# One core, a selective scan on VectorE: the product B x of the next step is issued ahead of the scan of this step

## Chip, cores and metric

The kernel runs on one core of one Trainium2 chip. The time is device time in microseconds (us) from launch to the last result, the median of several runs. Beside the times there is one profiled execution; its trace gives every instruction's start and duration on TensorE (PE), VectorE (DVE), ScalarE (ACT), GpSimd (POOL) and the DMA queues, counted from the start of the span.

## What is computed

Eight sequences of 512 tokens with 256 channels go through a state-space layer and then a layer of eight experts, all in float32. The part that matters is the scan of the first layer, for 512 inner channels and 16 state indices:

```python
dt = softplus(dt_in @ dt_proj_w.T + dt_proj_b)
A = -exp(A_log)
def step(state, inp):
    dt_t, B_t, C_t, x_t = inp
    state = exp(A[None] * dt_t[:, :, None]) * state + B_t[:, None, :] * x_t[:, :, None]
    y = einsum('bnd,bd->bn', state, C_t) + D * x_t
    return (state, y)
# x_t = silu(conv(layernorm(x) @ in_proj_w.T)); B, C, dt_in are projections of it
out = silu(y) @ out_proj_w.T + shortcut
# then: x1 = x + layernorm(out); x1 + layernorm(shared expert + chosen expert of layernorm(x1))
```

## The kernel before, in words

The 512 inner channels lie on 128 partitions in 4 chunks; time is the free dimension. The recurrence is independent for each channel and state index, so it is one scan instruction over time per (half of the channels, state index). I call one sequence a **pass**: 8 passes of Q = 32 **steps**, step q = (half q // 16, state index q % 16), each on tiles of 128 x 1024. Passes 0, 1, 6 and 7 are written out; passes 2 to 5 are two rounds of a dynamic loop with two passes each. For a step q:

- *decay q* (ACT, line 763, two instructions): exp(A dt) into PSUM, two buffers. It waits until scan q-2 is done.
- *product q* (B times x): 15 of 32 on POOL (line 500, the even q but 22), 17 on DVE (line 1078, the odd q and 22), into four buffers. DVE's product reads B from PSUM, where TensorE's *spread q* has put it over all partitions (line 1486, one buffer: spread q waits for the DVE product before it). POOL's product reads B from a tile loaded by DMA.
- *scan q* (DVE, line 1090): waits for product q, decay q, and for the state buffer of eight steps ago.
- *weighing q* (POOL, line 511): state times C, waits for scan q.
- *sum q* (TensorE, line 1529): adds weighed states in PSUM, waits for weighing q.

The order on each engine is written out by hand, per step q. On POOL: product q+4 if it is POOL's (it waits for scan q, because of the four buffers), then weighing q; at q = 20 also `loss` (line 516), a part of the softplus for the next pass. On ACT: decay q+2, then what the step has of other work. On TensorE: spread q+2, sum q-3, then other work.

The other work belongs to the next pass (`front`) and to the pass before (`back`). Of `front`: at q = 2, 4, 6, 8 ACT starts one convolution chunk (line 654), and at q = 3, 5, 7, 9 DVE adds its three taps (line 1025); at q = 10 ACT makes the SiLU behind decay 12; projections on TensorE at q = 11 and 14 (lines 1413, 1419); softplus on ACT at q = 12 to 22; at q = 23 and 24 DVE takes a minimum (line 1039) after ACT's square (line 688), which waits for `loss`; at q = 25 to 28 TensorE sums dt and ACT copies it (line 694). Of `back`: at q = 2 ACT copies y (line 753); at q = 15 and 17 TensorE does the output projection (line 1451), which waits for `front`'s projection to leave the bank; at q = 16 and 18 DVE adds it to the residual (line 1048) and takes statistics (line 1006). In pass 7 the shared expert of sequence 0 (`early`, lines 1507, 739, 1068) takes the place of `front`: its gate copies on ACT stand at q = 1 to 4, behind decay q+2. After pass 7 come the experts, which use none of this.

Of the kernel before, what the change touches and what calls it, by code (L numbers as in the profile page):

```python
# [19 lines left out]
def build(nc, x, winT, conv_w, xprojT, dt_w, dt_b, A_log, D, woutT, norm_w, norm_b,  # L20
# [47 lines left out]
    with ctx:  # L68
# [914 lines left out]
        def _(dve):  # L983
# [29 lines left out]
            def lead(f, par, q):  # L1013
                if q == 10:
                    dve.wait_ge(x_loaded, 16 * (f + 1))
                    if not (isinstance(f, int) and f < 2):
                        dve.wait_ge(mv_ready[0], f - 1)
                    stats(0, cl, f, xin, mv0[par], mv0_ready)

            def front(f, par, q):  # L1020
                if q in (3, 5, 7, 9):
                    c = q // 2 - 1
                    dve.wait_ge(tap_done, C * f + c + 1)
                    for m in range(1, TAPS):
                        last = nc.vector.scalar_tensor_tensor(  # L1025
                            out=acc[:, c, m:L], in0=psF[:, 0:L - m],
                            scalar=cw[:, c, TAPS - 1 - m:TAPS - m], in1=acc[:, c, m:L],
                            op0=ALU.mult, op1=ALU.add)
                        if m == TAPS - 1:
                            last.then_inc(conv_done, 1)  # L1030
                        else:
                            cf.link(f, last)
                if q in (23, 24):


                    h = slice(0, 2) if q == 23 else slice(2, 4)
                    dve.wait_ge(loss_ready, f + 1)
                    dve.wait_ge(sq_ready, f + 1)
                    nc.vector.scalar_tensor_tensor(out=lt[:, h], in0=lt[:, h], scalar=LN_MARGIN, in1=dt[par][:, h],
                                                   op0=ALU.add, op1=ALU.min).then_inc(min_done, 1)  # L1040

            def back(b, q):
                if q in (16, 18):
                    h = q // 2 - 8
                    dve.wait_ge(h0_ready, b + 1)
                    dve.wait_ge(oproj_ready, 2 * b + h + 1)
                    half = ao[:, 2 * h:2 * h + 2].rearrange("p a c -> p (a c)")
                    nc.vector.tensor_tensor(half, psF[:], half, ALU.add).then_inc(ao_done, 1)
                if q == 18:
                    dve.wait_ge(ao_done, 2 * b + 2)  # L1050
                    stats(1, cb, b, ao, mv[1], mv_ready[1])
                if q in (22, 24):
                    h = q // 2 - 11
                    if h == 0:
                        dve.wait_ge(xres_loaded, 16 * (b + 1))
                    dve.wait_ge(x1_normed, 2 * b + h + 1)
                    rows = slice(2 * h, 2 * h + 2)
                    nc.vector.tensor_tensor(ao[:, rows].rearrange("p a c -> p (a c)"), psF[:],
                                            xr[:, rows].rearrange("p a c -> p (a c)"),
                                            ALU.add).then_inc(x1_half, 1)  # L1060
                if q == 25:
                    dve.wait_ge(x1_half, 2 * (b + 1))
                    stats(2, cb, b, ao, mv[2], mv_ready[2])

            def early_act(c):
                dve.wait_ge(e_silu, 1)
                dve.wait_ge(e_up, c + 1)
                nc.vector.tensor_tensor(acc[:, c], psF[:], acc[:, c], ALU.mult).then_inc(e_act, 1)

            def choose(b):  # L1070
                dve.wait_ge(logit_ready, b + 1)
                nc.vector.tensor_copy(logits[:, bass.ds(b * J, J), :].rearrange("p j e -> p (j e)"),
                                      psF[:, 0:J * E]).then_inc(logit_kept, 1)

            def inject(i, par, q):
                h, n = divmod(q, N)
                dve.wait_ge(b_bcast, i * DQ + NTH_D[q] + 1)
                nc.vector.tensor_tensor(bx[q % RB][:], xh[par][:, h * CH:(h + 1) * CH],  # L1078
                                        psB[:].unsqueeze(1).broadcast_to([P, CH, L]), ALU.mult).then_inc(dve_bx, 1)

            def scan(i, q):
                k = i * Q + q
                if BY_POOL[q]:
                    dve.wait_ge(pool_bx, i * PQ + NTH_P[q] + 1)
                else:
                    dve.wait_ge(dve_bx, i * DQ + NTH_D[q] + 1)
                dve.wait_ge(decay_ready, k + 1)
                if not (isinstance(k, int) and k < RS):
                    dve.wait_ge(summed, k - RS + 1)
                nc.vector.tensor_tensor_scan(st[q % RS][:].rearrange("p c t -> p (c t)"),  # L1090
                                             decay[q % RD].rearrange("p c t -> p (c t)"),
                                             bx[q % RB][:].rearrange("p c t -> p (c t)"),
                                             0.0, ALU.mult, ALU.add).then_inc(scanned, 1)

            def iteration(i, par, do_lead, do_front, do_scan, do_back, do_choose=True):
                for q in range(Q):
                    if do_scan:
                        scan(i, q)
                        if q + 1 < Q and not BY_POOL[q + 1]:
                            inject(i, par, q + 1)  # L1100
                    if do_scan and not do_front and q in (12, 13, 14, 15):
                        early_act(q - 12)
                    if do_back:
                        back(i - 1, q)
                    if do_choose and q == 20:
                        choose(i - 2)
                    if do_front:
                        front(i + 1, 1 - par, q)
                    if do_lead:
                        lead(i + 2, par, q)  # L1110
# [42 lines left out]

            first_front()
            iteration(0, 0, True, True, True, False, False)
            iteration(1, 1, True, True, True, True, False)
            with dve.Fori(2, NB - 3, 2) as i:
                iteration(i, 0, True, True, True, True)
                iteration(i + 1, 1, True, True, True, True)
# [37 lines left out]
            oh, cnt, incl, q = rt["oh"], rt["cnt"], rt["incl"], rt["q"]  # L1197
# [543 lines left out]
```

## Time and profile before

| | us |
|---|---|
| median of 3 runs (1410.88 to 1412.58) | 1411.01 |
| the profiled execution, its time | 1411.09 |
| its span, first to last instruction | 1409.3 |
| busy PE / DVE / ACT / POOL | 1175.4 / 1089.8 / 770.9 / 1088.4 |
| DVE: 256 scans, 2279 ns each | 578.5 |
| DVE: 136 products, 1196 ns each | 162.7 |
| POOL: 256 weighings, 2398 ns each | 606.6 |
| POOL: 120 products, 2426 ns each | 291.1 |

DVE and POOL are busy in over nine tenths of nearly every slice from 45 to 992 us, the eight passes, and TensorE afterwards. A row of a timeline gives the start in us, the time to the end of the group in us, engine, line, operation, tile written and tiles read, and how many instructions are merged; in brackets, where the engine sat idle before it, how long and what ended that. Instructions of one engine overlap slightly: two scans in a row start 2.20 us apart.

### The profile page before, as it was taken

The page shows a single profiled execution, that of the slowest core. Times are in us where ns is not written, and L with a number is a line of the kernel's source. Part 1 is how long each engine was busy: PE and PEld are TensorE (multiplying, and loading weights), DVE is VectorE, ACT ScalarE, POOL GpSimd, SP SyncE. Part 2 cuts the span into 40 slices and gives each one's busy share as a digit, 9 for nine tenths or more (in the row PEclk, how much of TensorE's full clock was granted, in tenths as well). Part 3 has the DMA queues.
Part 4 walks back from the last instruction along what each step waited for, and adds up shares of the span by engine and source line. Part 5 has one row for each costly group of instructions (what it writes and reads, how often), then busy time and mean ns, then how long its engine had stood idle before and what let it go on. Part 6 is the DMA issues. An engine that isn't in the chain of part 4 may idle for free.

```text
span 1409.3 us, 15754 instructions
## 1 busy us (share of the span) xinstructions
PE 1175.4 (83%) x4782; PEld 518.5 (37%) x4783; DVE 1089.8 (77%) x1449; ACT 770.9 (55%) x1275; POOL 1088.4 (77%) x565
## 2 busy tenths in 40 slices
PE   5667678787886987888789688788999999999996
PEld 2222223222321422322233142233556655566653
DVE  3599999999999999999999989799241115776675
ACT  5757468676876866867686686556431111111111
POOL 0489999999999999999999999999122814444553
PEclk9898899999899999989998999999999999999998
DMA  3921211240150122014015012300269522222220
GB/s 108 274 68 62 90 60 32 75 150 0 65 192 1 62 91 106 32 75 149 1 66 175 1 62 90 134 0 31 90 238 324 162 71 82 81 81 79 83 67 15
DMA packets 72075, 127.71 MB, mean 91 GB/s; under 512 B 8759, under 2 KB 48448, under 8 KB 67904
## 3 DMA queue, kind: packets, MB, share of 16 engines
q1 hardware_dynamic: 60432, 103.72, 22.2%
q0 software_dynamic: 7152, 16.81, 3.7%
q10 hardware_dynamic: 4416, 6.29, 1.3%
q8 instruction: 33, 0.54, 0.2%
q14 instruction: 42, 0.34, 0.1%
HBM read 97.79 MB, written 31.76 MB: 92 GB/s over the span
## 4 chain that ended last, share of the span: by engine, by line
PE 36%; POOL 29%; issue 15%; DVE 12%; ACT 8%; DMA 0%; POOLq 0%; ACTq 0%; SPq 0%; DVEq 0%
POOL state L511 18%; PE psX L1647 10%; POOL bx L500 9%; DVE state L1090 6%; PE psX L1582 5%; PE psY L1595 3%; PE psY L1664 2%; PE bank L1664 2%; PE psY L1529 2%; PE bank L1451 2%; POOL lt L516 2%; ACT psX L763 2%; PE bank L1486 1%; DVE bx L1078 1%; DVE acc L1025 1%
## 5 line engine op out<-in xcount | busy, mean ns | idle before, releaser
L511 POOL TENSOR_TENSOR state<-state,cbc 128x1024 f32<-128x1024 f32 x256 | 606.6, 2398 | 14.9 <-DVE state L1090 14.8
L1090 DVE TENSOR_TENSOR_SCAN state<-psX,bx 128x1024 f32<-128x1024 f32 x256 | 578.5, 2279 | 38.5 <-ACT psX L763 23.1
L763 ACT ACTIVATE psX<-dt,aneg 128x511 f32<-128x511 f32 x512 | 330.7, 679 | 199.0 <-DVE state L1090 197.6
L500 POOL TENSOR_TENSOR bx<-xh,bbc 128x1024 f32<-128x1024 f32 x120 | 291.1, 2426 | 59.5 <-DMA bbc<-bc_rows 43.1
L1529 PE MATMUL psY<-state,ident 64*64 64x512 f32 x2048 | 287.5, 654 | 20.3 <-POOL state L511 20.0
L1486 PE MATMUL bank<-prow,ident 128*128 128x512 f32 x272 | 169.9, 710 | 113.3 <-DVE bx L1078 113.3
L1078 DVE TENSOR_TENSOR bx<-xh,bank 128x1024 f32<-128x1024 f32 x136 | 162.7, 1196 | 7.7 <-PE bank L1486 7.6
L1529 PEld LDWEIGHTS psY<-state,ident 64*64 64x64 f32 x2048 | 63.9, 140 | 206.8 <-issue 126.2
L961 ACT ACTIVATE sg<-psX 128x512 f32<-128x512 f32 x39 | 23.3, 597 | 196.5 <-PE psX L1647 196.5
L1486 PEld LDWEIGHTS bank<-prow,ident 128*128 128x128 f32 x272 | 48.0, 209 | 206.9 <-DVE bx L1078 166.9
L581 POOL DMA_INDIRECT ysl<-shared_rows,idx x39 | 40.3, 1033 | 80.6 <-DVE idx L1258 75.9
L1167 DVE TENSOR_TENSOR actS<-sg,psX 128x512 f32<-128x512 f32 x28 | 19.0, 686 | 103.6 <-ACT sg L911 103.6
L1647 PE MATMUL psX<-wg,xsT 128*128 x156 | 77.2, 617 | 1.3 <-DVE xsT L1243 0.6
L1647 PE MATMUL psX<-wu,xsT 128*128 x156 | 73.3, 592 | 0.0
L1406 PE MATMUL bank<-lt,win 128*128 128x512 f32 x112 | 55.5, 618 | 15.7 <-DVE acc L1025 14.4
L590 POOL DMA_INDIRECT result<-yo,idx x39 | 40.1, 1029 | 36.8 <-DVE yo L1306 29.3
L1025 DVE SCALAR_TENSOR_TENSOR acc<-bank,cw,acc 128x511 f32<-128x511 f32 (+2 forms) x84 | 62.3, 742 | 3.3 <-ACT acc L654 1.2
L561 POOL COPY xrow<-ids 128x4 f32<-128x4 f32 x8 | 1.6, 203 | 77.6 <-issue 55.1
L1249 DVE TENSOR_TENSOR actN<-sg,psX 128x512 f32<-128x512 f32 x39 | 26.8, 688 | 44.1 <-ACT sg L961 41.6
L1451 PE MATMUL bank<-wout,yv 128*128 128x256 f32 x256 | 58.5, 381 | 2.0 <-ACT yv L709 1.9
L911 ACT ACTIVATE sg<-psX 128x512 f32<-128x512 f32 x28 | 16.5, 596 | 76.8 <-PE psX L1582 76.8
L1582 PE MATMUL psX<-xg,shg 128*128 128x512 f32 x112 | 53.1, 596 | 1.8 <-DVE actS L1167 1.8
(200 smaller groups left out, 1718.8 us busy)
## 6 DMA issues: line engine op xcount, KB each, us to landing
cbc<-bc_rows SPq DMA_DIRECT2D x32, 1024.0 KB, 5.0
bbc<-bc_rows SPq DMA_DIRECT2D x16, 1024.0 KB, 6.2
slot_in<-ao SPq DMA_DIRECT2D x1, 5011.5 KB, 35.1
xsl<-slot_in SPq DMA_DIRECT2D x39, 128.5 KB, 2.0
xin<-in_x SPq DMA_DIRECT2D x8, 512.0 KB, 4.5
xr<-in_x SPq DMA_DIRECT2D x8, 512.0 KB, 5.5
x_rows<-ao SPq DMA_DIRECT2D x8, 512.0 KB, 2.9
xn_rows<-xr SPq DMA_DIRECT2D x8, 512.0 KB, 3.2
```

The costliest lines, as they stand in the source:

```text
L500: nc.gpsimd.tensor_tensor(bx[q % RB][:], xh[par][:, h * CH:(h + 1) * CH], bbc[:, n // 2].unsqueeze(1).broadcast_to([P, CH, L]), ALU.mult). ...
L511: nc.gpsimd.tensor_tensor(w[:], w[:], cbc[:, n].unsqueeze(1).broadcast_to([P, CH, L]), ALU.mult).then_inc(weighted, 1)
L763: e = nc.scalar.activation(decay[q % RD][:, c, 1:L], dt[par][:, h * CH + c, 1:L], ACT.Exp, scale=aneg[:, h * CH + c, n:n + 1])
L1025: last = nc.vector.scalar_tensor_tensor(out=acc[:, c, m:L], in0=psF[:, 0:L - m], scalar=cw[:, c, TAPS - 1 - m:TAPS - m], in1=acc[:, c, m:L ...
L1078: nc.vector.tensor_tensor(bx[q % RB][:], xh[par][:, h * CH:(h + 1) * CH], psB[:].unsqueeze(1).broadcast_to([P, CH, L]), ALU.mult).then_inc ...
L1090: nc.vector.tensor_tensor_scan(st[q % RS][:].rearrange("p c t -> p (c t)"), decay[q % RD].rearrange("p c t -> p (c t)"), bx[q % RB][:].rea ...
L1451: last = nc.tensor.matmul(psF[:, (j % 2) * DIM:(j % 2 + 1) * DIM], yv[:, c, j * P:(j + 1) * P], wout[:, c], start=(c == 0), stop=(c == C - 1))
L1486: nc.tensor.matmul(psB[:], ident[:, n:n + 1].broadcast_to([P, P]), prow[par][:], start=True, stop=True).then_inc(b_bcast, 1)
L1529: done = nc.tensor.matmul(psY[o * HP:(o + 1) * HP, r], weights(half, c), src[half, c], start=first, stop=last_)
L1582: last = nc.tensor.matmul(bank, w[:, k, c * P:(c + 1) * P], xg[g % 2][:, k], start=(k == 0), stop=(k == KC - 1))
L1647: last = nc.tensor.matmul(bank, xsT[i][:, k], w[:, bass.ds(ereg[i], 1), k].rearrange("p a n -> p (a n)"), start=(k == 0), stop=(k == KC - 1))
L1664: last = nc.tensor.matmul((psF, psG)[i][:, 0:DIM], actT[i][:, c], wd[:, bass.ds(ereg[i], 1), c].rearrange("p a n -> p (a n)"), start=(c == ...
```

## The change

For each step q that has a DVE product behind it, the product for step q+1 is put ahead of scan q instead of behind it. What follows scan and product in the step (`back`, `front`) stays behind both. The order was scan 0, product 1, scan 1, scan 2, product 3, scan 3; it becomes product 1, scan 0, scan 1, product 3, scan 2, scan 3. At q = 21 and 22 it becomes product 22, scan 21, product 23, scan 22.

```diff
             def iteration(i, par, do_lead, do_front, do_scan, do_back, do_choose=True):
                 for q in range(Q):
                     if do_scan:
-                        scan(i, q)
                         if q + 1 < Q and not BY_POOL[q + 1]:
                             inject(i, par, q + 1)
+                        scan(i, q)
                     if do_scan and not do_front and q in (12, 13, 14, 15):
                         early_act(q - 12)
                     if do_back:
```

## Rows read from the trace of the kernel before

**Rows 1.** Chain that ended last, shares of the span by engine.
```profile
PE 36%; POOL 29%; issue 15%; DVE 12%; ACT 8%; DMA 0%; POOLq 0%; ACTq 0%; SPq 0%; DVEq 0%
```
**Rows 2.** Who waited for whom, POOL for DVE: us in total, times, longest.
```profile
POOL bx L500 <- DVE state L1090: 16.4, 8, 5.6
POOL state L511 <- DVE state L1090: 14.8, 9, 3.0
```
**Rows 3.** Timeline of POOL, pass 3: weighing 19, product 24, `loss`.
```profile
484.32 2.35 POOL L511 TENSOR_TENSOR state<-state,cbc 128x1024 f32<-128x1024 f32 x1 [1.44 <-DVE state L1090]
486.64 2.35 POOL L500 TENSOR_TENSOR bx<-xh,bbc 128x1024 f32<-128x1024 f32 x1
...
491.26 4.54 POOL L516 TENSOR_TENSOR lt<-lt,dt 128x2048 f32<-128x2048 f32 x1
```
**Rows 4.** Chain that ended last, pass 5 to 6: start us, us, what.
```profile
726.65 4.56 POOL lt L516
...
804.92 0.67 ACT psX L763
...
837.89 2.36 POOL state L511
```
**Rows 5.** Timeline of DVE: product 11 and statistics; product and its scan, pass 6.
```profile
450.68 1.20 DVE L1078 TENSOR_TENSOR bx<-xh,bank 128x1024 f32<-128x1024 f32 x1
451.79 1.40 DVE L1006 BATCH_NORM_STATS2 bst<-xin 128x6 f32<-128x256 f32 x4
...
788.49 1.20 DVE L1078 TENSOR_TENSOR bx<-xh,bank 128x1024 f32<-128x1024 f32 x1
789.72 2.29 DVE L1090 TENSOR_TENSOR_SCAN state<-psX,bx 128x1024 f32<-128x1024 f32 x1
```
**Rows 6.** Timeline of DVE, pass 3: scans 0 to 3, product 3, first taps.
```profile
410.65 2.29 DVE L1090 TENSOR_TENSOR_SCAN state<-psX,bx 128x1024 f32<-128x1024 f32 x1 [1.25 <-ACT psX L763]
...
414.26 4.47 DVE L1090 TENSOR_TENSOR_SCAN state<-psX,bx 128x1024 f32<-128x1024 f32 x2 [0.21 <-DVE bx L1078]
418.65 1.20 DVE L1078 TENSOR_TENSOR bx<-xh,bank 128x1024 f32<-128x1024 f32 x1
420.05 2.29 DVE L1090 TENSOR_TENSOR_SCAN state<-psX,bx 128x1024 f32<-128x1024 f32 x1 [0.21 <-DVE bx L1078]
422.26 2.29 DVE L1025 SCALAR_TENSOR_TENSOR acc<-bank,cw,acc 128x511 f32<-128x511 f32 x3
```
**Rows 7.** Timeline of ACT, pass 3: decay 4, first tap's activation, decay 12.
```profile
418.76 1.30 ACT L763 ACTIVATE psX<-dt,aneg 128x511 f32<-128x511 f32 x2 [0.18 <-DVE state L1090]
...
421.16 0.69 ACT L654 ACTIVATE acc<-bank,cw 128x512 f32<-128x512 f32 x1
...
450.79 1.30 ACT L763 ACTIVATE psX<-dt,aneg 128x511 f32<-128x511 f32 x2 [3.10 <-DVE state L1090]
```
**Rows 8.** Timeline of PE: spread 31 of pass 2, spread 3 of pass 3.
```profile
404.32 1.02 PE L1486 MATMUL bank<-prow,ident 128*128 128x512 f32 x2
...
414.78 1.02 PE L1486 MATMUL bank<-prow,ident 128*128 128x512 f32 x2
```
**Rows 9.** Timeline of DVE, pass 3: scans 19 and 20.
```profile
481.99 4.43 DVE L1090 TENSOR_TENSOR_SCAN state<-psX,bx 128x1024 f32<-128x1024 f32 x2
```
**Rows 10.** Timeline of DVE, line 1039: the minimum in pass 0 and pass 3.
```profile
142.04 8.26 DVE L1039 SCALAR_TENSOR_TENSOR lt<-lt,dt 128x1024 f32<-128x1024 f32 x1 [1.13 <-ACT dt L688]
...
497.85 1.35 DVE L1039 SCALAR_TENSOR_TENSOR lt<-lt,dt 128x1024 f32<-128x1024 f32 x1 [0.34 <-ACT dt L688]
```
**Rows 11.** Timeline of DVE, pass 7: products 3 and 7.
```profile
891.81 1.22 DVE L1078 TENSOR_TENSOR bx<-xh,bank 128x1024 f32<-128x1024 f32 x1 [4.06 <-PE bank L1486]
...
906.17 1.22 DVE L1078 TENSOR_TENSOR bx<-xh,bank 128x1024 f32<-128x1024 f32 x1
```
**Rows 12.** Timeline of ACT, pass 7: decays 12 and 28.
```profile
917.55 1.30 ACT L763 ACTIVATE psX<-dt,aneg 128x511 f32<-128x511 f32 x2 [0.88 <-DVE state L1090]
...
974.22 1.30 ACT L763 ACTIVATE psX<-dt,aneg 128x511 f32<-128x511 f32 x2 [2.59 <-DVE state L1090]
```

## The prediction

> **What bounds the kernel now.** I read the chain that ended last first: its largest single engines are TensorE, then GpSimd [rows 1]. TensorE's share is mostly the expert part after 995 us, which the change does not touch, so only the eight passes of the scan (about 45 to 992 us) count. There the list of who waited for whom shows that GpSimd waits for VectorE for only 31 us in all [rows 2]: GpSimd's own work (weighings, its products, one `loss`) fills nearly the whole stretch, and a faster VectorE alone can win back no more than those 31 us.
>
> The question is what ends GpSimd's waits. In each of passes 1 to 6 there is one of 1.4 to 3.0 us in front of weighing 19; the shortest is shown [rows 3]. Weighing 19 waits for scan 19, product 24 behind it for scan 20, then comes weighing 20 and then `loss`. The chain shows, from pass 5 to pass 6, how this closes into a ring [rows 4]: from `loss` at 726.65 it leaves GpSimd, runs through ScalarE, TensorE and VectorE (softplus, dt, start of the pass, convolution taps, SiLU at 804.92, projections, statistics) and is back at weighing 19 at 837.89. So a pass lasts as long as this ring from `loss` to `loss`, and GpSimd's own work in it is 1.4 to 3.0 us shorter. Whatever moves a station of the ring moves the end, six times over.
>
> **The change.** It removes and adds no instruction: 136 products, 17 a pass, are issued one scan earlier. The scan that used to run ahead of such a product (the even ones, mostly) now runs behind it. No DMA moves, and no queue of SP or GpSimd changes. The product's own wait (for TensorE's spread of B) now stands ahead of the even scan, and behind that scan queue ScalarE's next decay, GpSimd's product q+4 and weighing q.
>
> (a) *What is saved.* Where the odd scan directly follows its own product, it starts 1.40 us after the product's start in the dynamic loop [rows 6] and 1.23 us in the passes written out [rows 5]. An instruction that doesn't need the product starts 1.11 us after it [rows 5]. In the new order the even scan follows and doesn't need it, so I take 1.40-1.11 = about 0.28 us saved per product in passes 2 to 5 and 0.12 in the others. The end on the other side is no saving at all: nothing in the trace shows a scan behind a product of another step. I take the saving because statistics behind a product, of which there is a row, stand nearest.
>
> The Trainium skill ("VectorE: DVE Perf Modes", section "The DRAIN you can't avoid") says that a semaphore after each VectorE instruction costs nothing extra, which would make (a) nil. The rows show 0.12 and 0.28 us, so I follow the rows; its case is a rival below.
>
> (b) *Scans 0 to 3 and the first tap, worked on pass 3.* At the end of pass 2, product 31 can start when its spread is there, 404.32+1.02 = 405.3 [rows 8]. Scan 30, which was done by then, must now follow: 405.4+1.1+2.2 = 408.7, scan 31 to 410.9, product 1 to 412.0, scan 0 to 414.2, scan 1 to 416.4. In the old order scan 1 ends at 416.45 (414.26+2.2, a pitch of two scans being 4.4) [rows 6]: equal, since product 1 fills part of the 1.25 us that scan 0 waited for ScalarE. Then product 3 (its spread is there at 415.8 [rows 8]) runs to 417.5 and scan 2 to 419.7, where it ended at 418.65. ScalarE's decay 4 waits for scan 2 and began at 418.76 [rows 7]; behind it in ScalarE's queue stand the copies of y and the first tap's activation at 421.16 [rows 7]. So decay 4 starts at 419.8, that activation ends at 422.9, and VectorE's first taps start there instead of at 422.26 [rows 6]: **+0.65 us**. Scan 3 ends 0.3 us earlier than before, which buys nothing. The same count in passes 1, 2, 4, 5 and 6 gives 0.2, 1.2, 0.87, 0.65 and 0.83, by how late the spread of step 3 is; together with pass 3 it is 4.4 us.
>
> (c) *Scan 10.* From the first taps to scan 10 VectorE has no idle time but the waits of (a); ScalarE's decay 12, ahead of SiLU in its queue, waits for scan 10 (3.10 us idle, 450.79 [rows 7]). Product 11 now stands ahead of scan 10: +1.11. Products 5, 7 and 9 give back 3 x 0.28 = 0.84, or 0.36 in the written-out passes 1 and 6. From there ScalarE and TensorE run without gaps to the projections, and scan 19 carries the shift: six times 1.11, less 4 x 0.84 + 2 x 0.36, is **+2.6 us**.
>
> (d) *Scan 20.* Scans 19 and 20 ran back to back from 481.99 [rows 9]; GpSimd took weighing 19 at 484.32 and product 24, which needs scan 20, at 486.64 without a gap [rows 3]. Now product 21 lies between: scan 20 ends 1.11+2.2 = 3.3 us behind scan 19, weighing 19 only 2.4 us: GpSimd waits **0.9 us** more, in each of six passes, 5.4 us. `loss` waits behind it, and the ring closes.
>
> (e) *From `loss` to the pass's end* I find nothing: the minimum (line 1039) still waits for ScalarE's square, which waits for `loss`; scan 23 ends about 0.8 us ahead of that, which is the cover. If it goes, the excess adds directly.
>
> (f) *Pass 0.* Scan 24 follows the long minimum of line 1039 [rows 10] and product 25 now stands ahead of it: GpSimd, which waits there, waits 1.1 us more. Its later waits in pass 1 (about 4 us, the one before weighing 19 among them) absorb that, and I count nothing; without this cover it is 1.1 us.
>
> (g) *Pass 7.* There TensorE is held by the shared expert's first matmuls, and products 3 and 5 wait for their spreads (4.06 us the first), and product 7 starts at 906.17 as its spread ends [rows 11]. Scans 2, 4 and 6 were done inside these waits; now each stands behind one. The spread of step 7 also slips by 0.8, since ScalarE's gate copy queues behind decay 4, which waits for scan 2. From product 7 on: 906.95 + 3 products (3.3) + 5 scans (11.0) = 921.3 for the end of scan 10, which was 917.4, just before decay 12 [rows 12]: +3.9. Decay 28, ahead of the last statistics, waits for scan 26 [rows 12], which has product 27 ahead of it now: +1.1, less 0.2 saved on the way. From there the tail (residual load, normalisation, experts) only shifts: **+4.8 us**.
>
> Sum: 4.4 + 2.6 + 5.4 + 4.8 = 17.2 us. The profiled execution has a span of 1409.3 and a time of 1411.09; the 1.8 us around the span stay, and the median of the runs is 1411.01, so either base gives **1428.2 us**. Shifts that I read to 0.5 us in seven passes, and (g), make its own range 1419 to 1437.
>
> **The rivals.** *No saving*: if the even scan starts as late behind a foreign product as the odd one does now, (c) grows by 4 x 0.84 + 2 x 0.36 = 4.1, and (g) by about half a us: 1433. The skill's rule on semaphores leads here.
>
> *Faster*: the ring is not what I take it for, and VectorE alone decides when scan 19 ends. It saves 17 times 0.12 to 0.28, 2 to 5 us a pass, more than the waits before weighing 19. These go, 13.8 us in passes 1 to 6: 1397. For it speaks that products now fill waits like the 1.25 us at 410.65 [rows 6]; against it that the chain of [rows 4] passes through ScalarE and TensorE.
>
> *Same*: (b) and (c) hit slack that the rows don't show, and (d) cancels against (a): 1411. Also here if the order of issue doesn't decide.
>
> *The port*: the minimum of line 1039 reads two tiles of SBUF. In pass 0 it took 8.26 us and ended only when GpSimd paused; in pass 3 it took 1.35 [rows 10]; once in seven passes it lost. The start against GpSimd's next instruction stays, as both follow from `loss`. But one more loss costs 8.26-1.35 = 6.9 us on the ring: 1435, two 1442; if pass 0's is won instead, GpSimd's waits behind it shrink by about 7: 1421.
>
> By the Trainium skill ("SBUF — State Buffer", section "SBUF: two separate sides") whoever starts first holds the pair for that whole instruction and the other blocks. Six of the seven agree; the 8.26 us in pass 0 spans more than one GpSimd instruction and doesn't.
>
> **How the numbers follow.** About 0.2% (2.8 us) is what a measurement of this kernel can tell from no change. Forecast 0.60; no saving 0.08; one or more further losses at the port 0.10; pass 0 won 0.05; same 0.07; faster 0.10. Hence slower 0.83, same 0.07, faster 0.10. The range runs from 1415 to 1440: it leaves out faster and same (0.17) and the worst port case.
>
> **What would show it.** Right: the wait before weighing 19 longer by 1 to 2 us in passes 1 to 6, and a new one of about 0.9 before product 24; ScalarE's wait for scan 10 longer by some 0.3 to 1.5; product to even scan 1.11 us; first taps waiting for ScalarE; in pass 7 scan 10 some 4 us later against its `loss`. Wrong: weighing 19 without a wait, or `loss` to `loss` shorter than now; or line 1039 over 5 us in a pass other than 0.

## The result, and the profile after the change

The changed kernel takes **1436.4 us** (median of 4 runs, 1431.07 to 1437.99) against 1411.62 us for the kernel before, measured beside it (4 runs): ratio 1.0168, 95% interval 1.0152 to 1.0183. It is slower, by 24.8 us; 17.2 us were forecast, with a range from 1415 to 1440. Its profiled execution took 1431.07 us, span 1429.3 us: 20.0 us more than the span of before.

The chain that ended last goes less through POOL and more through DVE than in [rows 1]:

```profile
PE 37%; POOL 21%; DVE 16%; issue 15%; ACT 10%; DMA 0%; POOLq 0%; DVEq 0%; ACTq 0%; SPq 0%
```

Who waited for whom (us in total, times, longest), as [rows 2]. POOL's products now wait for scans 30 times instead of 8; its weighings wait less:

```profile
POOL bx L500 <- DVE state L1090: 38.8, 30, 6.0
...
POOL state L511 <- DVE state L1090: 11.8, 7, 1.9
```

Timeline of POOL in pass 3 (start us, us, engine, line, operation, tiles, how many; in brackets the idle time before it and what ended that), as [rows 3]: product 18 now waits 1.11 us, the wait before weighing 19 went from 1.44 to 1.58 us, and there is a new one of 0.95 us before product 24:

```profile
472.05 2.35 POOL L500 TENSOR_TENSOR bx<-xh,bbc 128x1024 f32<-128x1024 f32 x1 [1.11 <-DVE state L1090]
...
489.92 2.36 POOL L511 TENSOR_TENSOR state<-state,cbc 128x1024 f32<-128x1024 f32 x1 [1.58 <-DVE state L1090]
493.23 2.36 POOL L500 TENSOR_TENSOR bx<-xh,bbc 128x1024 f32<-128x1024 f32 x1 [0.95 <-DVE state L1090]
...
497.88 4.51 POOL L516 TENSOR_TENSOR lt<-lt,dt 128x2048 f32<-128x2048 f32 x1
```

Pass 3 had the shortest of these waits. Over passes 1 to 6 the wait before weighing 19 was 2.98, 2.00, 1.44, 2.92, 1.59 and 2.90 us before and is 1.67, 1.64, 1.58, 1.68, 1.58 and 1.70 us now, 4.0 us less in all; what grew are the waits before products. In passes 2 to 6 alone the list of who waited for whom has for GpSimd, before (first line) and after (the other two):

```profile
POOL state L511 <- DVE state L1090: 11.2, 6, 2.9
...
POOL bx L500 <- DVE state L1090: 13.2, 15, 1.6
POOL state L511 <- DVE state L1090: 8.2, 5, 1.7
```

In these five passes GpSimd is busy for 576.4 us before and 576.9 after: its work is the same, and its waits grew by 10.2 us.

Timeline of DVE in pass 3, as [rows 5, 6] and [rows 10]: scan 2 starts 1.11 us behind product 3 (421.68 - 420.57), where a scan directly behind its own product needed 1.40; first taps now wait for ScalarE; and the minimum of line 1039 waits 1.79 us, where it was 0.34:

```profile
420.57 1.20 DVE L1078 TENSOR_TENSOR bx<-xh,bank 128x1024 f32<-128x1024 f32 x1
421.68 4.46 DVE L1090 TENSOR_TENSOR_SCAN state<-psX,bx 128x1024 f32<-128x1024 f32 x2
426.91 2.32 DVE L1025 SCALAR_TENSOR_TENSOR acc<-bank,cw,acc 128x511 f32<-128x511 f32 x3 [0.76 <-ACT acc L654]
...
504.44 1.34 DVE L1039 SCALAR_TENSOR_TENSOR lt<-lt,dt 128x1024 f32<-128x1024 f32 x1 [1.79 <-ACT dt L688]
```

Timeline of ACT, decay 12 of pass 3, as [rows 7]: it waits 4.24 us for scan 10 instead of 3.10:

```profile
455.75 1.30 ACT L763 ACTIVATE psX<-dt,aneg 128x511 f32<-128x511 f32 x2 [4.24 <-DVE state L1090]
```

To see where 20 us went I cut the ring at five places of the timelines: start of `loss`, first taps (line 1025), SiLU's table load (line 660), ScalarE's copy of the projection (line 671), weighing 19 ("w. 19"), and so on to the next `loss`. Each entry below is a difference of two such starts, in passes 2 to 6 summed over the five passes. Pass 7 is counted from the last `loss` to the first normalisation of the tail (line 631); what follows takes 414.3 to 414.6 us in every kernel. The other rows belong to the experiments (the line numbers in their traces are up to 9 higher than in the code above).

| profiled execution, us | `loss` of pass 0 | pass 1 | loss to taps | taps to SiLU | SiLU to copy | copy to w. 19 | w. 19 to `loss` | passes 2-6 | pass 7 | minimum, pass 0 | span |
|---|---|---|---|---|---|---|---|---|---|---|---|
| before | 135.4 | 121.8 | 242.9 | 148.9 | 82.8 | 78.4 | 34.7 | 587.6 | 150.2 | 8.26 | 1409.3 |
| after | 137.8 | 120.9 | 245.5 | 150.7 | 84.0 | 78.4 | 39.8 | 598.3 | 158.0 | 2.58 | 1429.3 |
| e1, after again | 138.3 | 121.0 | 245.5 | 150.7 | 84.0 | 78.4 | 39.7 | 598.4 | 160.6 | 2.52 | 1432.6 |
| e2, before, port | 134.9 | 116.2 | 243.2 | 148.9 | 82.8 | 78.4 | 34.7 | 588.0 | 149.8 | 1.35 | 1403.4 |
| e3, after, port | 138.0 | 122.3 | 244.6 | 150.8 | 84.6 | 78.4 | 39.7 | 598.0 | 158.8 | 1.23 | 1431.7 |
| e4, old step 10 | 136.2 | 123.1 | 242.9 | 145.1 | 82.8 | 78.4 | 39.7 | 588.8 | 155.8 | 6.94 | 1418.3 |
| e5, old step 20 | 138.7 | 119.9 | 252.4 | 150.7 | 84.4 | 78.4 | 34.7 | 600.6 | 163.8 | 2.52 | 1437.2 |
| e6, old step 2 | 138.4 | 124.2 | 240.3 | 150.7 | 88.3 | 78.4 | 39.7 | 597.4 | 158.7 | 7.13 | 1433.0 |
| e7, old pass 7 | 137.6 | 125.7 | 244.5 | 150.8 | 84.6 | 78.4 | 39.8 | 597.9 | 152.4 | 6.47 | 1428.1 |
| e8, mixed | 136.1 | 117.4 | 253.8 | 145.0 | 82.7 | 78.4 | 34.7 | 594.7 | 153.7 | 1.23 | 1416.3 |
| e9, TensorE busy | 136.4 | 124.2 | 246.4 | 150.7 | 82.7 | 78.4 | 39.7 | 597.9 | 158.8 | 7.00 | 1431.8 |
| e10, old 20 to 22 | 138.1 | 124.7 | 246.5 | 150.7 | 84.1 | 78.4 | 34.7 | 594.4 | 160.2 | 8.26 | 1431.7 |
| e11, new at 4, 6, 8 | 134.5 | 115.8 | 247.6 | 145.1 | 82.8 | 78.4 | 34.7 | 588.5 | 150.1 | 1.35 | 1403.3 |
| e12, e11 and busy | 136.4 | 116.0 | 236.9 | 145.2 | 82.7 | 78.4 | 34.7 | 578.0 | 149.7 | 1.37 | 1394.5 |

Of the 20.0 us, 2.4 fall on pass 0, -0.9 on pass 1, 10.7 on passes 2 to 6 and 7.8 on pass 7.

Two things of the table were in no step of the prediction. SiLU to copy grew by 1.2 us. And passes of the same code differ in length: 120.2, 119.0, 120.1, 118.9, 120.1 us in passes 2 to 6. The second is no effect of the change, for the kernel before does it too: 117.3, 116.7, 118.5, 116.9, 118.2 us. The timeline of PE shows both. In pass 3, two matmuls of line 1433 took 1.12 us (13.5 us behind `loss`) and the eight of line 1413 took 6.11; in pass 4 the former took 2.07, and the latter 5.40:

```profile
392.39 1.12 PE L1433 MATMUL bank<-acc,ident 128*128 128x512 f32 x2
...
460.32 6.11 PE L1413 MATMUL bank<-xh,xp 128*128 128x512 f32 x8 [3.61 <-ACT xh L660]
...
512.29 2.07 PE L1433 MATMUL bank<-acc,ident 128*128 128x512 f32 x2
...
581.05 5.40 PE L1413 MATMUL bank<-xh,xp 128*128 128x512 f32 x8 [2.97 <-ACT xh L660]
```

In the kernel before line 1433 took 1.12 us in pass 3 and 2.08 in pass 4, behind a gap of 3.31 us and a slow spread. It also had a long gap (4.97 us) near line 1413, but one spread and one sum ahead of it, and line 1413 took 4.38 us:

```profile
389.40 1.12 PE L1433 MATMUL bank<-acc,ident 128*128 128x512 f32 x2
...
451.93 2.08 PE L1486 MATMUL bank<-prow,ident 128*128 128x512 f32 x2 [4.97 <-DVE bx L1078]
...
455.85 4.38 PE L1413 MATMUL bank<-xh,xp 128*128 128x512 f32 x8
...
502.58 2.07 PE L1486 MATMUL bank<-prow,ident 128*128 128x512 f32 x2 [3.31 <-DVE bx L1078]
...
506.50 2.08 PE L1433 MATMUL bank<-acc,ident 128*128 128x512 f32 x2
```

The changed kernel's stretches of line 1433 by windows (window; length; busy us and instructions of PE, PEld, DVE, ACT, POOL; granted clock of TensorE, as a share of 2.4 GHz; DMA share; GB/s), 11 to 21 us behind `loss` of passes 2 and 3: the clock was 0.99 in one and 0.63 in the other.

```profile
390.00:400.00 10.00, 8.34 (x31) 2.91 (x30) 9.96 (x16) 3.45 (x6) 10.00 (x5) 0.99 0.43 157
...
509.00:519.00 10.00, 8.68 (x25) 2.84 (x25) 9.96 (x16) 3.54 (x6) 10.00 (x5) 0.63 0.45 161
```

### The profile page after: what moved, and what is told of

It reads as the page before. It is cut to its first block, busy times and chain, and to the rows that moved or that the text cites. A ratio compares the mean times of both kernels' runs of the same rounds, so it can differ in the third digit from the quotient of the medians.

```text
span 1429.3 us, 15754 instructions
## 1 busy us (share of the span) xinstructions
PE 1189.1 (83%) x4782; PEld 525.9 (37%) x4783; DVE 1079.1 (75%) x1449; ACT 772.6 (54%) x1275; POOL 1090.1 (76%) x565
## 4 chain that ended last, share of the span: by engine, by line
PE 37%; POOL 21%; DVE 16%; issue 15%; ACT 10%; DMA 0%; POOLq 0%; DVEq 0%; ACTq 0%; SPq 0%
POOL state L511 13%; PE psX L1647 10%; DVE state L1090 8%; POOL bx L500 7%; PE psX L1582 5%; ACT psX L763 3%; PE psY L1595 3%; DVE bx L1078 3%; PE psY L1664 2%; PE bank L1664 2%; PE psY L1529 2%; PE bank L1451 2%; DVE acc L1025 2%; POOL lt L516 1%; PE bank L1486 1%
## 5 line engine op out<-in xcount | busy, mean ns | idle before, releaser
L1486 PE MATMUL bank<-prow,ident 128*128 128x512 f32 x272 | 161.8, 679 | 39.4 <-DVE bx L1078 39.4
L1529 PEld LDWEIGHTS psY<-state,ident 64*64 64x64 f32 x2048 | 62.5, 138 | 251.3 <-POOL state L511 158.0
L1406 PE MATMUL bank<-lt,win 128*128 128x512 f32 x112 | 61.3, 674 | 20.2 <-DVE acc L1025 18.9
L1413 PE MATMUL bank<-xh,xp 128*128 128x512 f32 x56 | 39.9, 880 | 23.4 <-ACT xh L660 23.4
```

The source lines that it names most:

```text
L1406: last = nc.tensor.matmul(psF[:], win[:, k, c * P:(c + 1) * P], hT[:, k], start=(k == 0), stop=(k == KC - 1))
L1486: nc.tensor.matmul(psB[:], ident[:, n:n + 1].broadcast_to([P, P]), prow[par][:], start=True, stop=True).then_inc(b_bcast, 1)
L1529: done = nc.tensor.matmul(psY[o * HP:(o + 1) * HP, r], weights(half, c), src[half, c], start=first, stop=last_)
```

## Experiments

**e1, the changed kernel again**, to learn what sets its runs apart.

> The changed kernel once more, without an edit, to see in a profile what sets its four times apart (1431.07 us once, 1436.4 to 1438.0 three times). Port theory: the minimum of line 1039 in pass 0 sometimes takes about 8.3 us as in the kernel before, and sometimes 2.6 us as in the profiled execution of the changed kernel; a time of 1436 goes with the long one, a time of 1431 with the short one. Rival: the difference lies elsewhere, for instance in the clock of TensorE in pass 7; then a profile of about 1436 us shows the minimum of pass 0 at 2.6 us.

1434.37 us in the profiled execution and 1437.53 in another. The minimum of pass 0 took 2.52 us, as in the execution of 1431.07 us: so the port does not explain these 3.3 us. 2.6 of them lie in pass 7 (158.0 against 160.6 us). On PE's timeline the last down projection of the shared expert, 16 matmuls, took 3.69 us in the first execution, at a granted clock of 1.00, and 6.48 in this one, at 0.56:

```profile
999.10 3.69 PE L1519 MATMUL bank<-shd,acc 128*128 128x256 f32 x16 [2.61 <-ACT tmp L746]
```

```profile
999.52 6.48 PE L1519 MATMUL bank<-shd,acc 128*128 128x256 f32 x16 [4.14 <-ACT tmp L746]
```

**e2 and e3, the port of pass 0**, in the kernel before and in the changed one:

```diff
+                    if isinstance(i, int) and i == 0 and q == 22:
+                        pool.wait_ge(min_done, 3)
                     if BY_POOL[(q + RB) % Q]:
                         if q + RB < Q:
                             inject(i, par, q + RB)
```

> The kernel before, with one wait more: in pass 0 alone GpSimd starts its product 26 only when VectorE's minimum of line 1039 is through. Port theory: the minimum takes about 1.35 us as in passes 1 to 6 instead of 8.26; GpSimd waits up to 1.8 us for it, and the span is 4 to 6 us shorter: 1405 to 1407 us. Rival: the 8.26 us cost nothing because passes 1 and 2 absorb them, or the length comes from something other than GpSimd's access: 1411 us (or 1412 to 1413 with the wait as a cost).

**1405.0 us** against 1411.9 (ratio 0.996, 0.9948 to 0.9973); five of the seven runs lie at 1404 to 1405 us, two at 1409, and why those two is open. On the timelines of DVE and POOL in pass 0 the minimum takes 1.35 us and POOL waits 1.16 us for it:

```profile
141.49 1.35 DVE L1041 SCALAR_TENSOR_TENSOR lt<-lt,dt 128x1024 f32<-128x1024 f32 x1 [0.34 <-ACT dt L690]
```

```profile
142.92 2.35 POOL L500 TENSOR_TENSOR bx<-xh,bbc 128x1024 f32<-128x1024 f32 x1 [1.16 <-DVE lt L1041]
```

In the kernel before GpSimd did not pause beside the 8.26 us (142.04 to 150.30): a product and two weighings followed one another.

```profile
142.26 2.36 POOL L500 TENSOR_TENSOR bx<-xh,bbc 128x1024 f32<-128x1024 f32 x1
144.58 4.63 POOL L511 TENSOR_TENSOR state<-state,cbc 128x1024 f32<-128x1024 f32 x2
```

Pass 1 went from 121.8 to 116.2 us: the 8.26 us of [rows 10] were on the ring, and pass 1 did not absorb them.

> The same one wait in the changed kernel. Port theory: its times all come to that of the profiled execution with the short minimum, 1429 to 1432 us, none at 1436 to 1438. Rival (the spread of times has another cause): 1436 us as before, or both values again.

1432.8 us (1431.36 to 1434.06), 3.1 us below e1's median of the same chip. None of its runs reached 1435 us, but two lie above the expected 1429 to 1432, so the port is not the whole spread. The unchanged order's 5.6 us is not to be had here: pass 1 takes 122.3 us, although the minimum is short. What goes with that is that the minimum starts 8.4 us behind `loss` (6.6 in e2) and that the granted clock 10 to 22 us behind `loss` is 0.65 (0.74 in e2); no run separates the two. In e4, e6, e7, e9 and e10, all with the new order in pass 0 or most of it, the minimum took 6.5 to 8.3 us; in e5 and in both profiles of the changed kernel it took 2.5 to 2.6. So the race at the port is lost there in five profiles and won in three, and the profile of the changed kernel is one of the lucky ones. What its runs at 1436 to 1438 us had I can't say; they have no trace.

**e4, step 10 put back.**

```diff
-                        if q + 1 < Q and not BY_POOL[q + 1]:
-                            inject(i, par, q + 1)
-                        scan(i, q)
+                        scan_first = q == 10
+                        if scan_first:
+                            scan(i, q)
+                        if q + 1 < Q and not BY_POOL[q + 1]:
+                            inject(i, par, q + 1)
+                        if not scan_first:
+                            scan(i, q)
```

> The changed kernel with one step put back: at step 10 the scan stands ahead of product 11 again, in every pass. Ring theory: decay 12 and all behind it, up to scan 19, come 1.11 us earlier in passes 1 to 6, so that each of them is about 1.1 us shorter from one loss to the next (near 119.0 in place of about 120.1 us), 6 to 7 us in all, and with about 1 us in pass 7 the time is 7 to 8 us below the changed kernel's: 1428 to 1430 us. Rival (VectorE's whole work sets the pass, not the place of one scan): no change, 1436 us, passes as long as in the changed kernel.

**1421.4 us**, 14.6 us below e1: the direction was expected, the size was twice too small. Taps to SiLU fell by 1.13 us a pass (150.7 to 145.1), as expected, and by as much in passes 0 and 1. Beyond that SiLU to copy lost its 1.2 us, loss to taps came back to 242.9, and pass 7 gave 2.2 us. So this one scan costs 1.1 us a pass by itself, and in passes 2 to 6 some 0.8 us a pass more in the two stretches whose length goes with TensorE's clock.

**e5, step 20 put back**, as e4 with

```diff
+                        scan_first = q == 20
```

> The changed kernel with step 20 alone put back: scan 20 stands ahead of product 21 again, in every pass. Ring theory: the new wait of 0.95 us before product 24 goes, and weighing 19 to loss takes 6.94 us again in place of 7.95 in passes 1 to 6; all other stations of the ring stay, so that each pass is 1.0 us shorter and the time 6 us below the changed kernel's, 1429 to 1431 us. Rival (the wait only moves on, since the 1.8 us that VectorE's minimum of line 1039 now waits for ScalarE show that something behind loss has slack): weighing 19 to loss is shorter, but loss to the next first taps longer by the same, and the time stays at 1434 to 1437 us.

**1439.1 us**, above even the rival's range; the rival's mechanism holds. The wait before product 24 is gone (39.8 to 34.7 us), but loss to taps grew from 245.5 to 252.4. Against the changed kernel's profile that makes passes 2 to 6 2.3 us longer; 5.8 us more are in pass 7 (163.8 us): 1.8 are there when the first matmuls of line 1507 start (45.20 us behind `loss`, 43.39 in the changed kernel), the rest stays open. Timelines of DVE, ACT and POOL in pass 3 (`loss` starts at 498.32):

```profile
495.81 1.22 DVE L1078 TENSOR_TENSOR bx<-xh,bank 128x1024 f32<-128x1024 f32 x1 [1.12 <-PE bank L1490]
...
505.82 2.74 DVE L1039 SCALAR_TENSOR_TENSOR lt<-lt,dt 128x1024 f32<-128x1024 f32 x1 [0.50 <-ACT dt L688]
```

```profile
502.57 1.30 ACT L763 ACTIVATE psX<-dt,aneg 128x511 f32<-128x511 f32 x2 [1.03 <-DVE state L1090]
503.81 1.89 ACT L688 ACTIVATE dt<-tmp 128x2048 f32<-128x2048 f32 x1
```

```profile
505.11 2.36 POOL L500 TENSOR_TENSOR bx<-xh,bbc 128x1024 f32<-128x1024 f32 x1
507.43 5.65 POOL L511 TENSOR_TENSOR state<-state,cbc 128x1024 f32<-128x1024 f32 x2
```

Product 22 waits 1.12 us for its spread, ahead of scan 21; product 23 stands ahead of scan 22; decay 24 waits for scan 22, and the square of line 688, behind it, starts without waiting for `loss`. The minimum starts 7.5 us behind `loss`, not 6.6, in the middle of a GpSimd product, and ends 1.1 us after that: 2.74 us.

**e6, step 2 put back**, as e4 with

```diff
+                        scan_first = q == 2
```

> The changed kernel with step 2 alone put back: scan 2 stands ahead of product 3 again, in every pass. The prediction's step (b): decay 4, and with it the first tap's activation, no longer wait for product 3, so loss to first taps is 0.3 to 0.8 us shorter in passes 1 to 6 (about 0.25 by what the changed kernel's short passes show, 48.03 against 47.75 us). In pass 7 ScalarE's second gate copy, which stood behind decay 4, comes some 2 us earlier, and the spread of step 5 with it, so that pass 7 gives back 3 to 4 of its 7.8 us. In all 5 to 8 us below the changed kernel: 1428 to 1431 us. Rival (TensorE's granted clock alone sets loss to first taps, at 48.0 or 49.7 us, and the spread of step 5 in pass 7): loss to first taps stays at these two values, pass 7 keeps its 7.8 us, 1434 to 1437 us.

1435.2 us (1431.05 to 1436.55), not told apart from the changed kernel. Loss to taps fell by 5.2 us, to 48.1 us in every pass, and SiLU to copy grew by 4.3, to 17.6 in every pass: the alternation is gone and the gain with it. Pass 7 kept its 158.7 us. The rival was right on the time and on pass 7, though not on loss to taps staying at two values.

**e7, pass 7 in the old order**, as e4 with

```diff
+                        scan_first = isinstance(i, int) and i == NB - 1
```

> The changed kernel with pass 7 alone in the old order. Prediction's step (g), with the size that the trace of the changed kernel gives: the stretch from the last loss to the tail's first normalisation (150.2 us in the kernel before, 158.0 in the changed one) comes back to 150 to 151 us, and the time falls by 7 to 8 us or a little more: 1426 to 1430 us. Rival (what comes later in pass 7 is only an effect of where the last loss falls against TensorE's clock, not of the order): the stretch stays at 156 to 160 us, 1434 to 1437 us.

**1430.1 us**, 5 to 6 us less than the changed kernel. Pass 7 is back at 152.4 us, not quite at the expected 150 to 151; 2.2 of the 7.8 us remain, and they are there already when the first matmuls of line 1507 start (44.73 us behind `loss`, 42.45 in the kernel before). Products 3 and 5 wait as in [rows 11] (4.01 us the first), on DVE's timeline:

```profile
910.97 1.22 DVE L1078 TENSOR_TENSOR bx<-xh,bank 128x1024 f32<-128x1024 f32 x1 [4.01 <-PE bank L1490]
919.46 1.22 DVE L1078 TENSOR_TENSOR bx<-xh,bank 128x1024 f32<-128x1024 f32 x1 [2.76 <-PE bank L1490]
```

**e8, a mixture**: the wait of e2, and as e4 with

```diff
+                        scan_first = q in (2, 10, 20) or (isinstance(i, int) and i == NB - 1)
```

> A version made of both: in passes 0 to 6 the new order at all steps but 2, 10 and 20, which have the old one; pass 7 in the old order; and the one wait in pass 0 that lets the minimum go ahead of product 26. Ring theory with separate parts: against the kernel before with that wait (1405.0 us) the first taps come no later, first taps to SiLU's table load takes 29.0 us in place of 29.85 (29.39 in passes 1 and 6), and weighing 19 to loss 6.94 us: 4.2 us less, 1400 to 1402 us. Rival (the parts don't add up, since a pass that is shorter in one part finds TensorE at its lower clock in another): 1404 to 1408 us.

1418.7 us, slower than either theory gave. It has the short taps to SiLU (145.0) and weighing 19 to `loss` (34.7), but loss to taps takes 253.8: steps 21 and 22 keep the new order, and the minimum is late at the port as in e5 (2.4 to 3.5 us long in five of passes 1 to 6).

**e10, steps 20 to 22 put back**, to test that reading of e5:

```diff
+                        scan_first = q in (20, 21, 22)
```

> The changed kernel with steps 20, 21 and 22 put back, where the run with step 20 alone won 1.0 us ahead of loss and lost it behind it. Theory: there, ScalarE's square of line 688 had to wait for decay 24, which waits for scan 22, and scan 22 stood behind product 22, which waited 1.12 us for its spread, and behind product 23; so the minimum started 7.5 us behind loss in place of 6.6 and met GpSimd's next weighings at the port (2.74 us in place of 1.34). With scans 21 and 22 ahead of these products again, the square waits for loss alone, the minimum starts 6.6 us behind loss and takes 1.35 us, and loss to first taps stays at 48.0 or 49.8 us: passes 1 to 6 each 1.0 us shorter than the changed kernel's, 6 us in all, 1429 to 1431 us. Rival (whatever is won ahead of loss is lost behind it, since VectorE's work as a whole sets the pass): loss to first taps at 49 to 50.5 us in all passes, 1434 to 1439 us.

1431.3 us (1426.91 to 1433.62), at the upper edge of the expected 1429 to 1431; its profiled execution lost the race of pass 0 (8.26 us). The minimum takes 1.35 us in passes 1 to 6 and starts 6.6 us behind `loss`, weighing 19 to `loss` is back at 34.7, and loss to taps is 246.5 against e5's 252.4: that is the theory. Of its 5.1 us, 1.0 went to loss to taps and 0.1 to SiLU to copy, where the clock is.

**e9, TensorE kept busy** in the changed kernel. The added matmuls multiply a state tile by a quarter of the identity that holds only zeros and add that to the sum:

```diff
+                for _ in range({20: 3, 11 - SUM_LAG: 2}.get(q, 0)):
+                    tiles(st[q % RS], lambda half, c: ident[half, HP - half.start:P - half.start], False, False)
                 tiles(st[q % RS], lambda half, c: ident[half, half], False, n == N - 1).then_inc(summed, 1)
```

> The changed kernel with matmuls added that add zeros to the sum: 24 ahead of sum 20, in the 4.9 us in which TensorE waits for GpSimd's loss, and 16 ahead of sum 8, in the 3.6 us in which it waits for SiLU. Clock theory: the passes of the changed kernel alternate between about 120.1 and 118.9 us because TensorE is at its lower clock either 10 to 20 us behind loss (line 1433 takes 2.07 us there, not 1.10, and first taps come 49.8 us behind loss, not 48.0) or around line 1413 (6.1 us; SiLU's table load to the copy of line 671 is 17.2 us, not 16.55). With TensorE kept at work both go: 48.0 and 16.55 us in each of passes 2 to 6, each about 118.4 us, and 3 to 7 us less in all: 1429 to 1433 us. Rival (the alternation comes from elsewhere, for instance from the phase of DMAs or of the loop): passes go on alternating, 1434 to 1438 us.

1433.9 us (1432.45 to 1436.19), between the expected 1429 to 1433 and the rival's 1434 to 1438: half of the theory fell. The eight matmuls of line 1413 took 3.70 us in every pass, in pass 3 with 2.89 us of idle time still before them, and SiLU to copy is 16.55 us in every pass. But first taps came 49.1 to 49.5 us behind `loss` in every pass, not 48.0: the granted clock is 0.50 (1.2 GHz) 12 to 16 us behind `loss`, each time:

```profile
462.83 3.70 PE L1413 MATMUL bank<-xh,xp 128*128 128x512 f32 x8 [2.89 <-ACT xh L660]
```

```profile
392.00:396.00 4.00, 3.54 (x10) 1.14 (x11) 4.00 (x4) 0.81 (x2) 4.00 (x3) 0.50 0.36 131
...
511.70:515.70 4.00, 3.46 (x10) 1.14 (x11) 4.00 (x3) 0.82 (x3) 4.00 (x3) 0.50 0.37 133
```

The low clock had only moved: in the changed kernel it was 0.99 there in pass 3 and 0.63 in pass 4. A gap filled in one place leaves the next one.

**e11, the new order where nothing waits for the displaced scan**: the wait of e2, and as e4 with

```diff
+                        scan_first = q not in (4, 6, 8) or (isinstance(i, int) and i == NB - 1)
```

> The new order only at steps 4, 6 and 8 of passes 0 to 6, where a product and a scan follow one another with nothing else waiting for that scan; the old order at all other steps and in pass 7, and the one wait in pass 0 that lets the minimum go ahead of product 26. Theory: nothing late is added at any station of the ring, and the three products give back their 0.28 us: first taps to SiLU's table load takes 29.0 us in place of 29.85 (29.39 in passes 1 and 6), and all other stations stay as in the kernel before with that wait (1405.0 us): 4 us less, 1400 to 1402 us. Rival (a shorter stretch shifts where TensorE stands at its lower clock, and gives it back there): 29.0 us in that stretch, but 1403 to 1407 us.

**1405.0 us** (ratio 0.9953, 0.9934 to 0.9971): faster than before, but no faster than e2. Taps to SiLU is 3.8 us shorter than in e2, as worked out, and loss to taps 4.4 us longer: the rival. On PE's timeline in pass 3 (`loss` at 485.64) a gap of 3.31 us is followed by matmuls at half speed (granted clock 0.50), the spread with 2.08 us and line 1433 (here 1439) with 2.00:

```profile
492.56 1.09 PE L1535 MATMUL psY<-state,ident 64*64 64x512 f32 x8 [1.27 <-POOL state L511]
496.96 2.08 PE L1492 MATMUL bank<-prow,ident 128*128 128x512 f32 x2 [3.31 <-DVE bx L1080]
...
500.88 2.00 PE L1439 MATMUL bank<-acc,ident 128*128 128x512 f32 x2
```

**e12, e11 with these gaps filled**: the matmuls of e9, 8 ahead of sum 20, 24 ahead of sum 21 and 16 ahead of sum 29, in passes 0 to 6:

```diff
+                if not (isinstance(i, int) and i == NB - 1):
+                    for _ in range({20: 1, 21: 3, 29: 2}.get(q, 0)):
+                        tiles(st[q % RS], lambda half, c: ident[half, HP - half.start:P - half.start], False, False)
```

> The version with the new order at steps 4, 6 and 8 of passes 0 to 6 and the one wait in pass 0, and with it matmuls that add zeros to a sum in the three gaps of TensorE that its trace shows ahead of the slow matmuls: 8 ahead of sum 20, 24 ahead of sum 21 (3.3 us idle behind it) and 16 ahead of sum 29 (2.5 us idle), in passes 0 to 6. Clock theory: the low clock follows these gaps, so that line 1433's first matmuls take 1.1 us in place of 2.0 and first taps come 47.7 to 48.0 us behind loss in every pass in place of 49.1 to 49.9; each of passes 2 to 6 takes 116.0 to 116.5 us in place of 117.3 to 118.1, and the time is 7 to 10 us below 1405.0: 1395 to 1398 us. Rival (the lower clock only moves to another stretch of the ring, as it did when the gap ahead of line 1413 was filled): first taps come no earlier or another station comes later by as much, 1402 to 1408 us.

**1396.1 us** (1394.07 to 1396.84; ratio to the kernel before 0.9887, 0.987 to 0.9903). First taps come 47.4 us behind `loss` in each of passes 2 to 6, and each takes 115.5 to 115.6 us. The same place on PE's timeline (`loss` at 483.51), and POOL's weighing 19:

```profile
490.43 3.66 PE L1535 MATMUL psY<-state,ident 64*64 64x512 f32 x32 [0.42 <-POOL state L511]
494.83 1.12 PE L1492 MATMUL bank<-prow,ident 128*128 128x512 f32 x2 [0.73 <-DVE bx L1080]
...
497.08 1.12 PE L1439 MATMUL bank<-acc,ident 128*128 128x512 f32 x2
```

```profile
476.56 2.36 POOL L511 TENSOR_TENSOR state<-state,cbc 128x1024 f32<-128x1024 f32 x1 [0.23 <-DVE state L1092]
```

With 48 matmuls more per pass that compute nothing, the spread takes 1.12 us instead of 2.08 and the kernel is 9 us faster. The granted clock thus decides loss to taps; and the wait before weighing 19, GpSimd's only one in passes 2 to 6, is down to 0.2 or 0.3 us, so now GpSimd's own work bounds the pass. No run has these matmuls with the old order at steps 4, 6 and 8; what the new order adds at a steady clock is therefore not measured, though taps to SiLU is 3.7 us shorter than in e2 (145.2 against 148.9).

## Why the prediction was right, and where it was not

The direction and the mechanism hold: a displaced scan is late at the ring, six times over. One of the signs did not come. The wait before weighing 19 was to grow by 1 to 2 us; it shrank in four of the six passes and changed by at most 0.14 us in the others, because GpSimd now waits earlier, before product 18 above all, for the displaced scan 14. The ring shows in GpSimd's waits as a whole, 10.2 us more in passes 2 to 6, which are 10.7 us longer. And the row at 804.92 [rows 4], which the prediction reads as SiLU, is decay 12; SiLU follows directly behind it. By its steps:

- **(a)** is right: product to foreign scan is 1.11 to 1.14 us in the dynamic loop and in the passes written out. The case of no saving falls. The rule of the Trainium skill ("VectorE: DVE Perf Modes", section "The DRAIN you can't avoid") that a semaphore costs nothing extra, measured there on copies, does not hold for this pair of instructions: the product's own scan starts 1.40 us behind it [rows 6].
- **(b)** named the right wait (first taps wait 0.76 us for ScalarE), but its sizes were too large: in pass 3, which it works out, loss to taps went from 47.72 to 48.02 us, 0.30 more and not 0.65. In passes 2 to 6 it grew by 2.6 us, not 4.2, and 1.7 of these are pass 2 alone (48.25 to 49.91 us), where the granted clock 10 to 21 us behind `loss` fell from 0.74 to 0.60. Undoing step 2 took 5.2 us off this stretch and put 4.3 on SiLU to copy (e6). What ends the stretch late is mostly TensorE's clock, which the working took as fixed.
- **(c)** has its size: taps to SiLU grew by 1.9 us in passes 2 to 6; the terms give 4 x 0.27 + 0.75 = 1.83. But its consequence stopped short. That TensorE runs "without gaps to the projections" is the sentence that failed: the kernel before had a gap of 4.97 us there already, and the later scan puts one of 3.61 us directly before line 1413, where the granted clock is now 0.60 instead of 0.84 (pass 3). The slow matmuls add 1.2 us. e4 has no gap before line 1413 and gets the 1.2 us back; it shows that step 10 is worth 14.6 us of the 24.8.
- **(d)** is right in place and size (0.95 us before product 24, 5.1 us in five passes against 4.5), but it isn't separate from (e).
- **(e)** came out at nothing, as forecast, but only because (d) hides what it overlooked. Scan 23 is not the cover: VectorE sits idle for 0.34 us before the minimum in pass 3 [rows 10], not 0.8. The cover lies on ScalarE, whose square stands behind decay 24, and that waits for scan 22. In the kernel before, on ACT's timeline:

```profile
495.83 1.91 ACT L688 ACTIVATE dt<-tmp 128x2048 f32<-128x2048 f32 x1 [0.89 <-POOL lt L516]
```

With (d) alone taken away `loss` comes 1 us earlier, product 22 waits 1.12 us for its spread, and it and product 23 stand ahead of scan 22: the square no longer waits for `loss`, and the minimum loses at the port (e5). With steps 20 to 22 taken away together it does not (e10).
- **(f)** failed: pass 0 was 2.4 us later at its `loss` already (0.6 at the first taps, 1.3 at SiLU, 1.8 at the copy), where the working looked only at scan 24. The shifts of (b) and (c) act there as well (e4: 1.6 us of it).
- **(g)** was mis-sized: 7.8 us, not 4.8. Up to SiLU's table load it came to 7.2 us instead of 3.9. The step that failed is the slip of 0.8 us for the spread of step 7: it slipped by 4.2 us, and the other 3.1 of the 3.9 us came as worked out. Timelines of ACT, PE and DVE in pass 7 after the change:

```profile
909.23 1.30 ACT L763 ACTIVATE psX<-dt,aneg 128x511 f32<-128x511 f32 x2 [4.49 <-DVE state L1090]
...
911.43 0.59 ACT L739 ACTIVATE acc<-bank 128x512 f32<-128x512 f32 x1
```

```profile
912.07 3.53 PE L1507 MATMUL bank<-xin,shg 128*128 128x512 f32 x4 [2.38 <-ACT acc L739]
```

```profile
905.78 1.22 DVE L1078 TENSOR_TENSOR bx<-xh,bank 128x1024 f32<-128x1024 f32 x1 [7.03 <-PE bank L1486]
916.65 1.22 DVE L1078 TENSOR_TENSOR bx<-xh,bank 128x1024 f32<-128x1024 f32 x1 [5.27 <-PE bank L1486]
```

Decay 4 waits 4.49 us for scan 2, which stands behind the late product 3; the gate copy behind it lets the next matmuls of line 1507 start 2.5 us later against `loss` than before, these take 3.53 us instead of 1.98, and the spread of step 5 stands behind them. e7 confirms the cause (the order in pass 7) for 5.6 of 7.8 us; e6 shows that scan 2 alone is not it.

- **The port** was a rival with 0.10 for losing and 0.05 for winning pass 0. In the profiled execution pass 0 was won, which took 3.7 us off loss to taps of pass 1; no race was lost in passes 1 to 6. Without that the profiled execution would stand near 1435 us, 1.6 us short of the median.

So the sum for passes 2 to 6 (10.7 against 10.5) came near partly by luck: an overestimate of 1.6 us in (b) met 1.2 us of the clock in SiLU to copy and 0.6 more in (d). The miss of 7.6 us against the median is (g) with 3, (f) with 2.4, and the rest in the spread that e1 shows; how the latter divides between clock and port in the unprofiled runs stays open.

## What to carry to other kernels

Moving work ahead of an instruction that others wait for costs up to its full length at each place where that wait is on the path, and saves only the small bubble it fills: do it step by step, where nothing waits (here steps 4, 6 and 8), not everywhere. A late instruction also opens gaps in TensorE, and the slow matmuls behind such a gap can cost nearly as much again; look at the granted clock of the stretch before counting a TensorE stretch as fixed. If a pass is bounded by such a ring, matmuls that add zeros in the gaps may win more than any reordering; here they won 8.9 us (e11 to e12), and little where only some gaps were filled (e9).

## What the runs showed of the hardware

TensorE's granted clock falls to 0.50 (1.2 GHz) in stretches behind idle time of the engine (3.31 us in e11), and these stretches differ from pass to pass: passes of the same code took 120.1 and 118.9 us in turn. The Trainium skill ("TensorE: Matmul & The Clock Gate", section "HAM oscillation — how this bites in real kernels") describes kernels in which waits between groups of matmuls throttle TensorE again and again, and advises a loop order that keeps it at work; the runs agree, and show that filler does it as well (1405.0 to 1396.1 us).

A VectorE instruction that reads two tiles of SBUF beside a busy GpSimd can lose several turns in a row: the 8.26 us of [rows 10] span three GpSimd instructions, the 2.74 us of e5 only the rest of one. One wait on GpSimd's side, which cost it 1.16 us, made the kernel 6.9 us faster.
